# Blocks' first entries read from the input, histogram ahead of the first norm, first chunk's indices loaded by themselves

## The chip, the cores and the metric

One core of a Trainium2 chip runs the whole program. The metric is device time in microseconds. A profiled execution has a time of its own, and all rows shown here come from that one. The engines are TensorE (PE), VectorE (DVE), ScalarE (ACT), GpSimd (POOL) and SyncE (SP). Each has its own instruction stream, and they meet at semaphores. SP, ACT and POOL start DMAs.

## The reference

The input is a table x of 6250 nodes by 256 features and a graph of 206250 edges (src, dst), sorted by dst. One layer is computed:

```python
xn = layernorm(x)
q, k, v = xn @ Wq.T + bq, xn @ Wk.T + bk, xn @ Wv.T + bv      # 8 heads of 32
for every node c: softmax over its edges (r -> c) of q[c] . k[r] / sqrt(32), times v[r], summed
x = x + agg @ Wo.T + bo + linear_attention(xn) @ w_out.T + b_out
x = x + mixture_of_experts(layernorm(x))      # 8 experts, top 1, capacity 977
```

The edge weights are not used.

## The kernel before

Nodes stand in 49 tiles of 128. Edges, padded, stand in 1664 blocks of 128 entries; the 1612 blocks that hold real edges fill dst_d and src_d, copies of the lists in device memory.

**Front.** Each tile of x is normed, transposed, and multiplied by the key, value and query weights. The keys and values go to the table kv_d, one row of 520 numbers per node. Beside that the kernel sorts the nodes by their number of edges, and it does so in steps:

- SP copies dst into dst_d (L273), adds the padding (L276, L277), waits for both (L281) and reads the first entry of every block back into fi_i, 13 columns of 128 (L282). Then come the third group of x rows (L284), weights, and the copy of src.
- DVE norms the first seven tiles (L331), then makes a histogram of the first entries (L342 to L370), with matmuls on PE between. From it L412 gets for every node the block in which its edges begin.
- POOL reads that block for each node: 49 indirect DMAs (L417), which wait for L412 and for dst_d. DVE counts in four portions (L426 to L435) how many entries lie before the node. A portion is taken up when the tile loop has come to the tile in `ROWS_AT`; if its rows have not landed, DVE stands. Then POOL reads the first 64 source indices of each node from src_d, 49 indirect DMAs (L438).
- DVE and PE work out each node's place in the order of degree (L442 to L518). POOL scatters each node's query and indices to that place in qs_d, 49 indirect DMAs (L405), tile c after the query of tile c has been made (L782).

The generator `ranks` holds these steps, and the tile loop (L727) takes two steps of it per tile. After the loop, weights for the second attention are centred (L803).

**Loop.** The sorted tiles are handled in chunks of up to 8 edges per node. A ring of 6 buffers takes the gathered rows. For each chunk POOL issues up to 8 indirect DMAs (L1028) after ACT has copied its indices to ixb (L1091 for the first six, L1164 later) and after PE has freed a buffer (e_fr; L1022). DVE multiplies keys by the query (L1391), sums (L1394), later weighs the values (L1425). PE adds them (L1323) and frees the buffer. ACT does the exponentials (L1175, L1176). In the first stretch of the loop PE and ACT also carry the second attention: PE's first matmul of that part (L1239, keys_values(0, 0)) stands ahead of its first L1323, and it needs xw, a tile of xn_d.

**Between.** When all scatters to qs_d have landed, SP's list is, in this order: the indices of the first 13 tiles (L959), their queries (L960), the 36 other tiles in three DMAs of 1920 KB (L962), 3 numbers of every row for all tiles (L963, 6272 pieces of 12 bytes), and then the first three tiles of xn_d (L969). The last part of the file is the mixture of experts.

Of the kernel before, what the change touches and what calls it, by code (L numbers as in the profile page):

```python
# [16 lines left out]
J = 8  # L17
RING = 6
# [12 lines left out]
QI = 320  # L31
SW = 323
WIDE = 50 * QI + 4 * J * ROW
ROWS_AT = (7, 13, 20, 25)
PUMP = 2
EPS = 1e-5
BIG = 1e30
# [32 lines left out]
def gps_layer_kernel(nc, x, src, dst, wall, ball, wmix, wqm, wout, wo, bo, b_out, gate_w, gate_b, w1, b1, w2, b2, out):  # L70
# [3 lines left out]
    i32 = mybir.dt.int32  # L74
# [5 lines left out]
    V, S, T, G, Y = nc.vector, nc.scalar, nc.tensor, nc.gpsimd, nc.sync  # L80

    ctx = ExitStack()
    with ctx:
        sems = {}

        def sem(name):
            sems[name] = Sem(ctx.enter_context(nc.semaphore(name)))
            return sems[name]
# [12 lines left out]
        def take(n):  # L101
            top[0] += n
            assert top[0] <= 53008 - WIDE, top[0]
            return A[:, top[0] - n:top[0]]

        def r3(ap, b):
            return ap.rearrange("p (a b) -> p a b", b=b)

        def dram(name, shape, dt=f32):
            return nc.dram_tensor(name, shape, dt, kind="Internal").ap()  # L110
# [3 lines left out]
        qs_d = dram("qs_d", [NP, SW])  # L114
        dst_d = dram("dst_d", [NBP, 128], i32)
# [7 lines left out]
        wait = Waits()  # L123
# [7 lines left out]
        def g(ins):  # L131
            return sg.inc(ins)

        def dma(eng, o, i, s, **kw):
            return s.inc(eng.dma_start(o, i, **kw), 16)
# [35 lines left out]
        ixb = [take(J).bitcast(i32) for _ in range(RING)]  # L171
# [13 lines left out]
        def temp(n):  # L185
            pre[0] += n
            assert pre[0] <= 2048
            return R3[:, pre[0] - n:pre[0]]
# [12 lines left out]


        S.preload_act_table_set("natural_log_exp_and_others")
        t_c = g(G.memset(ident, 0.0))
        t_c1 = g(G.memset(tri, 1.0))
        t_c2 = g(G.memset(ones, 1.0))
# [32 lines left out]
        xbuf = [r3(R2[:, o:o + 1792], 256) for o in (12352, 6400, 8192)]  # L239
# [11 lines left out]
        t_x = {0: load_x(0, S)}  # L251
# [8 lines left out]
        t_x[1] = load_x(1, S)  # L260


        s_pad, s_ed, s_fi = sem("s_pad"), sem("s_ed"), sem("s_fi")
        zero = R3[:, 2048:2176]
        blank = R3[:, 3136:3136 + 4 * HR]
        bigi = R3[:, 128:256].bitcast(i32)
# [9 lines left out]
        dma(Y, flat(dst_d)[E:E + 86].rearrange("(a b) -> a b", a=1), bigi[0:1, 0:86], s_ed)  # L276
        t_ed = dma(Y, dst_d[NB:NBP, :], bigi[0:NBP - NB, :], s_ed)  # L277
        assert E + 86 == NB * 128
        firsts = temp(13)
        fi_i = temp(13).bitcast(i32)  # L280
        wait(Y, t_ed)  # L281
        t_fi = dma(Y, fi_i, dst_d.rearrange("(a p) j -> p a j", p=128)[:, :, 0], s_fi, allow_slow_non_contiguous=True)  # L282

        t_x[2] = load_x(2)  # L284
        s_w2 = sem("s_w2")
# [14 lines left out]
        def spread(xt, js):  # L300
            for i in js:
                last = v(V.bn_stats(st[:, 6 * i:6 * i + 6], xt[:, i, :]))
            wait(V, last)
            for i in js:
                v(V.bn_aggr(mv[:, 2 * i:2 * i + 2], st[:, 6 * i:6 * i + 6]))
# [6 lines left out]
        def root(n):  # L312
            wait(S, (sv, sv.n))
            return inverse_root(rs[:, 0:n], r3(mv, 2)[:, 0:n, 1])
# [7 lines left out]
        def norm(xt, n, o=None):  # L322

            spread(xt, range(n))
            wait(V, root(n))
            for i in range(n):
                last = center(xt, i, o)
            return last

        wait(V, t_x[0])  # L330
        t_n = {(0, 6): norm(xbuf[0], 7)}  # L331


        NB13 = 13
        hs = R0[:, 3584:5120]
# [84 lines left out]
        def ranks():  # L420
            for i, (c0, c1) in enumerate(QUARTERS):
                while tile[0] < ROWS_AT[i]:
                    yield
# [251 lines left out]

        wait(V, t_w)
        v(V.tensor_scalar(out=W[:, :, 512:768], in0=W[:, :, 512:768], scalar1=32.0 ** -0.5, scalar2=None, op0=ALU.mult))
        t_bl = v(V.tensor_scalar(out=bal[:, 512:768], in0=bal[:, 512:768], scalar1=32.0 ** -0.5, scalar2=None, op0=ALU.mult))  # L680
# [46 lines left out]
        for t in range(NT + 3):  # L727
            tile[0] = t
            grp, j = divmod(t, 7)
# [39 lines left out]
            if 0 <= t - 2 < NT:  # L769
                u = t - 2  # L770
                b0, b1_ = ps[2 * (u % 2)], ps[2 * (u % 2) + 1]
# [6 lines left out]
            if 0 <= t - 3 < NT:  # L778
                u = t - 3
                b0, b1_ = ps[2 * (u % 2)], ps[2 * (u % 2) + 1]  # L780
# [71 lines left out]
        e_arr = [esem(f"arr{i}") for i in range(RING)]  # L852
# [5 lines left out]
        e_xs, e_ix, e_q = [esem(n) for n in ("xs", "ix", "q")]  # L858
# [1 line left out]
        e_kv, e_ke, e_k1, e_k2, e_k3, e_ks, e_kz, e_dz, e_wm = [esem(n) for n in  # L860
            ("kv", "ke", "k1", "k2", "k3", "ks", "kz", "dz", "wm")]
        e_xw = [esem(f"xw{i}") for i in range(3)]
        s_in = [sem(n) for n in ("s_ids", "s_first", "s_others", "s_sorted3")]
        sortedi = r3(sorted3.bitcast(i32), 3)
        s_ag = sem("s_ag")
        e_so, e_si, e_sa, e_sd, e_se, e_sl, e_sg = [esem(n) for n in ("so", "si", "sa", "sd", "se", "sl", "sg")]
# [82 lines left out]
        def _(e):  # L949
            p, u, bs, last = regs(e, "y_", ["p", "u", "bs", "last"], [0, 0, 0, 0])  # L950
# [5 lines left out]

            e.wait_ge(s_q.h, s_q.n)
            some_rows = lambda a_, b_, c0, c1: qs_d[a_ * 128:b_ * 128, c0:c1].rearrange("(t p) w -> p t w", p=128)
            s_in[0].inc(e.dma_start(qi[:, 0:FIRST, 256:QI], some_rows(0, FIRST, 256, QI)), 16)  # L959
            s_in[1].inc(e.dma_start(qi[:, 0:FIRST, 0:256], some_rows(0, FIRST, 0, 256)), 16)  # L960
            for c0, c1 in ((FIRST, 25), (25, 37), (37, NT)):
                s_in[2].inc(e.dma_start(qi[:, c0:c1, :], some_rows(c0, c1, 0, QI)), 16)  # L962
            s_in[3].inc(e.dma_start(r3(sorted3, 3), some_rows(0, NT, QI, SW), allow_slow_non_contiguous=True), 16)  # L963
# [116 lines left out]
        def _(e):  # L1080
# [4 lines left out]
            e.nop().then_inc(e_bc, 1)  # L1085
            e.nop().then_inc(e_ks, 1)
            e.wait_ge(sv.h, t_rg[0][1])
            e.wait_ge(s_in[0].h, 16)
            for k in range(RING):
                e.reg_load(ix_, nsl[0:1, 52 + k:53 + k])  # L1090
                e.activation(ixb[k], ixf[:, bass.ds(val(e, ix_, NT * QI + 320 - J), J)], ACT.Copy).then_inc(e_ix, 1)  # L1091
            e.wait_ge(sv.h, t_wm[1])
# [775 lines left out]
```

## Time and profile before

| | us |
|---|---|
| median of 3 runs | 2860.02 (2859.44 to 2861.61) |
| the profiled execution | 2859.73 |
| its span, first to last instruction | 2858.5 |
| outside the span | 1.2 |

| stage | from, us | to, us |
|---|---|---|
| front: tiles, histogram, order | 0 | 212.6 |
| from the last scatter to the first gather | 212.6 | 219.8 |
| gathers | 219.8 | 2291 |
| scatters of the attention's output | 2291.6 | 2354.2 |
| mixture of experts | 2354.2 | 2858.5 |

A row of the timeline gives the start, the duration, the engine, the line, what is done to which tensor, and in brackets how long the engine was idle before it and what ended that. The waits view sums such idle times by the line that waited and what it waited for: the total, the number, the longest. A view of one line gives the shortest, median and longest time of its DMAs from issue to landing. The DMA view splits a stretch by queue: q1 is SP's, q10 is ACT's, q0 is POOL's.

### The profile page before, as it was taken

What the parts mean: (1) busy time and instruction counts of PE and PEld (TensorE: products, weight loads), DVE (VectorE), ACT (ScalarE), POOL (GpSimd) and SP (SyncE); (2) the same over time, 40 slices, a digit from 0 to 9 for tenths busy, and PEclk for the clock granted to TensorE, in tenths of its full rate; (3) what the DMA queues carried; (4) which work ended last, traced back from release to release, by engine and by line L of the source; (5) the groups of instructions that cost most, each with busy time, mean ns of one, the idle gap of its engine ahead of it and who ended that gap; (6) DMA issues with size and microseconds to landing.
All of it is one profiled execution on the core that took longest, in us unless ns stands there. A gap on an engine that the chain in (4) does not pass through costs nothing. (4 is left out here: it accounts for less than half of the span.)

```text
span 2858.5 us, 36150 instructions
## 1 busy us (share of the span) xinstructions
PE 2101.6 (74%) x9360; PEld 1688.3 (59%) x9361; DVE 2399.5 (84%) x3265; ACT 1026.7 (36%) x4371; POOL 2104.4 (74%) x2222
## 2 busy tenths in 40 slices
PE   6872777777877777777888766666566537599998
PEld 5752665655666565555666554444444427499997
DVE  6774999988989999999999888899999956366765
ACT  3422666665666666211111110101111105335453
POOL 5776777777777777777777777777777775578785
PEclk9985999999889999889999887878887875699999
DMA  7759777777777777878888877777777749333331
GB/s 248 270 206 294 221 219 217 219 217 218 219 217 219 218 219 216 244 231 258 256 256 256 252 223 212 210 211 211 210 211 211 211 154 293 118 76 89 80 90 15
DMA packets 257843, 586.96 MB, mean 205 GB/s; under 512 B 49474, under 2 KB 135569, under 8 KB 257613
## 3 DMA queue, kind: packets, MB, share of 16 engines
q0 software_dynamic: 150448, 467.11, 58.2%
q1 hardware_dynamic: 98027, 109.52, 11.6%
q10 hardware_dynamic: 9296, 9.44, 1.0%
q8 instruction: 37, 0.61, 0.1%
q14 instruction: 35, 0.29, 0.0%
HBM read 519.06 MB, written 71.84 MB: 207 GB/s over the span
## 5 line engine op out<-in xcount | busy, mean ns | idle before, releaser
L1028 POOL DMA_INDIRECT wide<-kv_d,arena x1099 | 1051.3, 957 | 347.4 <-issue 326.1
L1323 PE MATMUL ps<-wide,arena 128*128 128x264 f32 x2432 | 706.8, 454 | 229.2 <-DVE wide L1425 229.0
L1323 PEld LDWEIGHTS ps<-wide,arena 128*128 128x128 f32 x2432 | 539.4, 227 | 389.5 <-DVE wide L1425 273.7
L1028 POOL DMA_INDIRECT arena<-kv_d,arena x539 | 515.7, 957 | 164.3 <-issue 157.9
L1161 ACT ACTIVATE ps<-wide 128x256 f32 x229 | 88.7, 387 | 1262.0 <-DVE arena L1391 1258.3
L1394 DVE TENSOR_REDUCE arena<-arena 128x64 f32<-128x2048 f32 x229 | 523.9, 2288 | 7.9
L1323 PE MATMUL ps<-arena 128*128 128x264 f32 x1216 | 345.7, 446 | 135.0 <-DVE arena L1425 134.9
L1391 DVE TENSOR_TENSOR arena<-wide,ps 128x2048 f32<-128x2048 f32 x153 | 349.4, 2284 | 88.0 <-DMA wide<-kv_d,arena 87.7
L1323 PEld LDWEIGHTS ps<-arena 128*128 128x128 f32 x1216 | 264.3, 222 | 211.8 <-DVE arena L1425 157.4
L140 PE MATMUL ps<-halves 128*128 128x256 f32 (+2 forms) x2304 | 362.1, 319 | 3.1 <-DVE halves L1686 1.6
L1425 DVE TENSOR_TENSOR wide<-wide,ps 128x2112 f32<-128x2112 f32 x152 | 356.8, 2347 | 0.0
L140 PEld LDWEIGHTS ps<-halves 128*128 128x128 f32 x2304 | 331.7, 192 | 31.0 <-POOL halves L1696 3.4
L1239 PE MATMUL ps<-arena 128*128 128x256 f32 x528 | 136.4, 404 | 98.4 <-DMA arena<-xn_d 52.0
L1391 DVE TENSOR_TENSOR arena<-arena,ps 128x2048 f32<-128x2048 f32 x76 | 173.5, 2284 | 34.3 <-DMA arena<-kv_d,arena 34.1
L1131 ACT ACTIVATE arena<-arena 128x64 f32<-128x64 f32 x784 | 197.8, 334 | 3.2
L1425 DVE TENSOR_TENSOR arena<-arena,ps 128x2112 f32<-128x2112 f32 x76 | 178.4, 2347 | 16.2 <-ACT arena L1176 16.2
L1123 ACT ACTIVATE arena<-arena 128x64 f32<-128x64 f32 x784 | 188.7, 242 | 3.1
L1239 PEld LDWEIGHTS ps<-arena 128*128 128x128 f32 x528 | 99.7, 199 | 117.9 <-DMA arena<-xn_d 53.5
L1792 DVE TENSOR_TENSOR halves<-arena,halves 128x978 fp32r<-128x978 f32 x64 | 97.9, 1539 | 65.8 <-ACT halves L1790 65.8
L1123 ACT ACTIVATION_READ_ACCUMULATOR arena<-arena 128x1 f32 x784 | 146.2, 186 | 0.0
L1831 POOL DMA_INDIRECT out<-arena x48 | 80.1, 1668 | 78.3 <-DVE arena L1828 37.8
L140 PE MATMUL ps<-rear_halves,row_halves 128*128 128x512 f32 (+1 forms) x392 | 113.0, 361 | 14.2 <-DVE wide L785 13.1
(337 smaller groups left out, 3079.2 us busy)
## 6 DMA issues: line engine op xcount, KB each, us to landing
wide<-kv_d,arena POOLq DMA_INDIRECT x1099, 3.8
arena<-in_w SPq DMA_DIRECT2D x16, 1024.0 KB, 5.5
kv_d<-wide SPq DMA_DIRECT2D x49, 260.0 KB
arena<-xn_d SPq DMA_DIRECT2D x82, 128.0 KB, 3.5
arena<-kv_d,arena POOLq DMA_INDIRECT x539
hb_d<-arena SPq DMA_DIRECT2D x16, 516.0 KB, 6.7
xn_d<-arena SPq DMA_DIRECT2D x7, 896.0 KB
base_d<-arena ACTq DMA_DIRECT2D x49, 128.0 KB, 3.4
```

The costliest lines, as they stand in the source:

```text
L140: m = T.matmul(o, l, r, start=(first and i == 0), stop=(last and i == len(pairs) - 1))
L1028: e.indirect_dma_start(out=kvb[k][:, j, :], out_offset=None, in_=kv_d, in_offset=bass.IndirectOffsetOnAxis(ap=ixb[k][:, j:j + 1], axis=0)) ...
L1123: m = e.activation(o[:, 64 * h:64 * h + 64], raw[:, 64 * h:64 * h + 64], ACT.Square, accum_out=ssq[:, h:h + 1])
L1131: m = e.activation(o[:, 64 * h:64 * h + 64], raw[:, 64 * h:64 * h + 64], ACT.Copy, scale=rr_[:, h:h + 1])
L1161: return e.activation(q_ps, qsf[:, bass.ds(val(e, qa, NT * QI), 256)], ACT.Copy)
L1239: m = e.matmul(o, xw_[slot][:, i, :], W0[:, i, c:c + 256], start=(i == 0), stop=(i == 1))
L1323: m = e.matmul(psE[(k + 1) % 3][:, 0:264], ident, kvb[b][:, j, 256:ROW], start=(j == 0), stop=(j == J - 1))
L1391: e.tensor_tensor(prod.rearrange("p (j n) -> p j n", n=256), kvb[k][:, :, 0:256], q_ps.unsqueeze(1).to_broadcast([128, J, 256]), ALU.mult) ...
L1394: e.tensor_reduce(S_ps[:, 0:8 * J], prod.rearrange("p (n d) -> p n d", d=32), AX.X, ALU.add).then_inc(e_red, 1)
L1425: e.tensor_tensor(kvv[b], kvv[b], p3.unsqueeze(3).to_broadcast([128, J, 8, 33]), ALU.mult).then_inc(e_pv, 1)
L1792: t_hs[e * 8 + f] = v(V.tensor_tensor(hl[:, f, 0:CE], hf[f % 2], hh[:, f, 0:CE].bitcast(f32), ALU.subtract))
L1831: t_yq[q] = s_ye[q % 4].inc(G.indirect_dma_start(out=out, out_offset=bass.IndirectOffsetOnAxis(ap=rows_[:, jj % 4, 256:257].bitcast(i32), ...
```

## The change

fi_i is filled from the input dst itself: POOL first sets it to 2^20, SP waits for that, and three DMAs with 1536, 75 and 1 entries are the first on SP's list, ahead of the copy to dst_d. SP no longer waits for dst_d. The norm of the first seven tiles stands behind the histogram on DVE. The portions of `ROWS_AT` are taken up at tiles 5, 10, 16 and 21. In the loop's head SP loads the 8 indices of chunk 0 by themselves straight into ixb[0], and ACT only passes the word on. SP then waits until chunk 0's 8 gathers have landed, before it loads the 36 other tiles.

```diff
-ROWS_AT = (7, 13, 20, 25)
+ROWS_AT = (5, 10, 16, 21)
...
+        firsts = temp(13)
+        fi_i = temp(13).bitcast(i32)
+        s_fi = sem("s_fi")
+        t_fm = g(G.memset(fi_i, 1 << 20))
+        wait(Y, t_fm)
+        first_of = lambda b0, n: dst[b0 * 128:(b0 + n) * 128]
+        dma(Y, fi_i[:, 0:12], first_of(0, 12 * 128).rearrange("(a p j) -> p a j", p=128, j=128)[:, :, 0], s_fi, allow_slow_non_contiguous=True)
+        dma(Y, fi_i[0:75, 12:13], first_of(1536, 75).rearrange("(p j) -> p j", j=128)[:, 0:1], s_fi, allow_slow_non_contiguous=True)
+        t_fi = dma(Y, fi_i[75:76, 12:13], dst[206208:206209].rearrange("(a b) -> a b", a=1), s_fi)
         t_c = g(G.memset(ident, 0.0))
...
-        firsts = temp(13)
-        fi_i = temp(13).bitcast(i32)
-        wait(Y, t_ed)
-        t_fi = dma(Y, fi_i, dst_d.rearrange("(a p) j -> p a j", p=128)[:, :, 0], s_fi, allow_slow_non_contiguous=True)
...
-        wait(V, t_x[0])
-        t_n = {(0, 6): norm(xbuf[0], 7)}
-
...
+        wait(V, t_x[0])
+        t_n = {(0, 6): norm(xbuf[0], 7)}
         wait(V, t_w)
...
             some_rows = lambda a_, b_, c0, c1: qs_d[a_ * 128:b_ * 128, c0:c1].rearrange("(t p) w -> p t w", p=128)
+            s_in[4].inc(e.dma_start(ixb[0], qs_d[0:128, 256:256 + J].bitcast(i32)), 16)
             s_in[0].inc(e.dma_start(qi[:, 0:FIRST, 256:QI], some_rows(0, FIRST, 256, QI)), 16)
             s_in[1].inc(e.dma_start(qi[:, 0:FIRST, 0:256], some_rows(0, FIRST, 0, 256)), 16)
+            e.wait_ge(e_arr[0], 16 * J)
...
+            e.wait_ge(s_in[4].h, 16)
+            e.nop().then_inc(e_ix, 1)
             e.wait_ge(s_in[0].h, 16)
-            for k in range(RING):
+            for k in range(1, RING):
```

## Rows read from the trace of the kernel before

**Rows 1.** Waits of POOL, whole span: line and what it waited for, total, times, longest

```profile
POOL wide L1028 <- issue: 326.1, 1070, 0.3
...
POOL wide L1028 <- PE ps L1323: 11.3, 19, 5.8
```

**Rows 2.** Timeline of POOL at the places where its run of DMAs starts, breaks and ends

```profile
22.23 1.29 POOL L417 DMA_INDIRECT arena<-dst_d,arena  x1 [17.65 <-DVE arena L413]
...
211.60 0.97 POOL L405 DMA_INDIRECT qs_d<-wide,arena  x1 [0.30 <-issue]
219.80 0.99 POOL L1028 DMA_INDIRECT wide<-kv_d,arena  x1 [7.23 <-ACT arena L1091]
...
268.93 0.95 POOL L1028 DMA_INDIRECT wide<-kv_d,arena  x1 [0.30 <-issue]
275.72 0.95 POOL L1028 DMA_INDIRECT wide<-kv_d,arena  x1 [5.84 <-PE ps L1323]
...
2353.19 0.97 POOL L1075 DMA_INDIRECT at_d<-wide,arena  x1 [0.30 <-issue]
```

**Rows 3.** Timeline from 262 us to 277 us, the loop's head: first of PE, then DVE

```profile
266.33 3.78 PE L1239 MATMUL ps<-arena 128*128 128x256 f32 x8 [51.96 <-DMA arena<-xn_d]
...
276.07 2.35 DVE L1425 TENSOR_TENSOR arena<-arena,ps 128x2112 f32<-128x2112 f32 x1 [16.18 <-ACT arena L1176]
```

**Rows 4.** Timeline of the first 23 us: waits and ends of norm and histogram

```profile
6.84 2.39 DVE L302 BATCH_NORM_STATS2 arena<-wide 128x6 f32<-128x256 f32 x7 [0.83 <-DMA wide<-in_x]
...
10.45 3.11 DVE L319 TENSOR_SCALAR wide<-wide,arena 128x256 f32<-128x256 f32 x7 [0.61 <-ACT arena L310]
11.49 0.40 SPq L135 DMA_DIRECT2D arena<-dst_d  x1
...
15.16 0.17 DVE L343 TENSOR_SCALAR arena<-arena 128x13 int32<-128x13 int32 x1 [1.60 <-DMA arena<-dst_d]
...
21.86 0.42 DVE L679 TENSOR_SCALAR wide<-wide 128x512 f32<-128x512 f32 x1
```

**Rows 5.** Timeline around the rows of the first nodes and the last query

```profile
68.77 0.39 DVE L767 TENSOR_TENSOR row_halves<-arena,row_halves 128x256 fp32r<-128x256 f32 x1
...
71.67 0.95 POOL L417 DMA_INDIRECT arena<-dst_d,arena  x1 [0.31 <-issue]
...
201.50 0.38 ACT L782 ACTIVATE wide<-ps 128x256 f32<-128x256 f32 x1 [2.21 <-PE ps L140]
```

**Rows 6.** Timeline from 214 us to 235 us: first loads, first indices, first product

```profile
214.19 0.37 SPq L959 DMA_DIRECT2D wide<-qs_d  x1
...
215.44 18.63 SPq L962 DMA_DIRECT2D wide<-qs_d  x3
218.70 0.21 ACT L1091 ACTIVATE arena<-wide 128x8 int32 x1 [16.81 <-DMA wide<-qs_d]
...
234.69 2.29 DVE L1391 TENSOR_TENSOR arena<-wide,ps 128x2048 f32<-128x2048 f32 x1 [20.09 <-DMA wide<-kv_d,arena]
```

**Rows 7.** Issue to landing: L1028, L417, L962

```profile
DMA to landing us min/median/max: 3.4/3.8/6.6
...
DMA to landing us min/median/max: 2.4/5.0/7.2
...
DMA to landing us min/median/max: 18.7/28.5/35.2
```

**Rows 8.** DMA by queue, 4 us each from 216, 220, 232, 256: packets, MB, share

```profile
q1 hardware_dynamic: 2183, 1.27, 111.6%
...
q1 hardware_dynamic: 1274, 1.42, 108.6%
...
q0 software_dynamic: 255, 0.86, 57.6%
q1 hardware_dynamic: 514, 0.65, 46.7%
...
q1 hardware_dynamic: 3304, 0.06, 48.4%
```

More of the change, by code:

```diff
@@ L260, in gps_layer_kernel @@
         t_x[1] = load_x(1, S)
-        s_pad, s_ed, s_fi = sem("s_pad"), sem("s_ed"), sem("s_fi")
+        s_ed = sem("s_ed")
         zero = R3[:, 2048:2176]
@@ L862, in gps_layer_kernel @@
         e_xw = [esem(f"xw{i}") for i in range(3)]
-        s_in = [sem(n) for n in ("s_ids", "s_first", "s_others", "s_sorted3")]
+        s_in = [sem(n) for n in ("s_ids", "s_first", "s_others", "s_sorted3", "s_ids0")]
         sortedi = r3(sorted3.bitcast(i32), 3)
```

## The prediction

> **What bounds the kernel now.** I first ask which engine never rests, and read the waits of POOL over the whole span. Nearly all its idle time in the gathers is "issue", never longer than 0.3 us at a time; the one long wait for PE is the 5.8 us inside 19 waits of 11.3 us in all [rows 1]. So the gathers are a run of 1638 DMAs, one each 1.26 us, which nothing but a late start or a break can lengthen. The timeline of POOL shows where the run starts and breaks [rows 2]: it starts at 22.23 with the first row gather, goes on without a gap through 3 x 49 DMAs to 211.60 + 0.97, stands 7.23 us, does 40 gathers (five chunks) from 219.80 on, stands 5.84 us before 275.72, and then runs to 2353.19 + 0.97, beyond which the experts follow. There are three idle pieces: 22.2 us, 7.2 us and 5.8 us. The change works on the first two.
>
> The third decides whether that counts. At 268.93 POOL issues the last gather of chunk 4, and the sixth chunk's buffer must be freed by PE. So I go to what PE waits for in the loop's head: its first L1239 starts at 266.33 after 51.96 us of waiting for a tile of xn_d [rows 3]. PE's list has that matmul ahead of the first L1323, so no buffer is freed until it is done. From 266.33 it is 9.39 us to POOL's restart at 275.72, and 9.74 us to DVE's L1425 at 276.07, which had stood 16.18 us behind ACT's L1176, which is behind the same matmul [rows 2, 3]. The tile of xn_d is the last thing on SP's list, behind 5.90 MB of sorted tiles. Everything ahead of 266.33 is thus covered by that load: the time moves by what the landing of that load moves, and by nothing else that happens before.
>
> **The change, part by part.**
>
> *First entries and histogram.* Before, DVE stands 1.60 us for fi_i and begins the histogram at 15.16; POOL starts 7.07 us later, at 22.23 [rows 2, 4]. After, the three small DMAs are SP's first. The trace has none like them; the old read took 15.16 - 11.49 = 3.67 us from issue with 1664 such entries [rows 4], and the x rows, issued at about 0.9, were used from 6.84 with the same neighbours. Issued at 1.3 to 2.5, the third lands between 2.5 + 3.67 = 6.2 and some 8. DVE's constants end at 6.0, so I take 6.5. Then POOL starts at 6.5 + 7.07 = 13.57, 8.66 us earlier. It also needs dst_d, which landed by 11.49 [rows 4]; its copy is now behind three DMAs of about 0.4 us issue each, so 11.5 to 13, hidden by the 13.57. The memset ahead of POOL's constants costs 0.1 to 0.2 us, hidden under the same wait. Behind SP's removed wait stood the third x group, the weights and the copy of src; they go out some 4 us earlier beside x group 1, and none is waited for then. Between gain and loss of 1 us: 0.
>
> *Norm behind the histogram.* The norm takes 10.45 + 3.11 - 6.84 = 6.72 us, of which 0.61 is ACT's root. It now ends at about 13.3 + 6.7 = 20.0, and L679 comes at 20.1 instead of 21.86: the two idle pieces of DVE, 0.83 and 1.60, are gone, less 0.7 [rows 4]. The tiles come 1.8 us earlier, or 0 to 1.8.
>
> *ROWS_AT.* The rows must have landed when the tile loop comes. The tightest is tile 16: before, DVE came there after the L767 at 68.77, now at about 67.4; the 39th row gather went out at 71.67, now at 63.0, and lands 5.0 (median) to 7.2 us later, 68.0 to 70.2 [rows 5, 7]. DVE may stand 0.6 to 3 us. Behind it on DVE are the tiles. The last query was done at 201.9 [rows 5]; with -1.8 and up to +3 it is at 200 to 203, and the last scatter, now due at 211.60 - 8.66 = 202.94, has it, or waits at most 0.4. The later portions are ready long before POOL comes to them. Cost 0.
>
> *Chunk 0's indices.* From L959 to ACT's L1091 it was 4.51 us with 416 KB, and POOL came 1.10 later; 214.19 is 2.59 us after the last scatter's issue [rows 2, 6]. With 4 KB the landing is no longer than that, and no shorter than the 2.4 us of the fastest row gather [rows 7]. I take 3.0, a saving of 1.5 (0 to 2.1), nearer the lower end because the load is tiny. The other five chunks' indices are copied by 211 and wanted at 219. First gather: 202.94 + 2.59 + 3.0 + 1.1 = 209.6 instead of 219.80.
>
> The Trainium skill, "DMA: Bandwidth & Descriptors", section "Anatomy of one DMA", gives a small DMA a fixed time of about 2.0 us. No row here shows so short a landing, 2.4 being the least; by the page the first gather would be 1 us earlier and so would everything behind it.
>
> *The wait for chunk 0.* SP now holds its list until 8 gathers have landed. The eighth goes out 7 x 1.257 + 0.06 = 8.86 us after the first. Before, DVE had it at 234.69, which is 6.0 us after 219.80 + 8.86, beside the tile loads [rows 2, 6]; the median of all gathers is 3.8 [rows 7]. So the wait ends at 209.6 + 8.9 + 3.8 = 222.3, and DVE's first product comes there instead of 234.69 [rows 6]. Behind the wait are queued: the 36 tiles, the 3 numbers per row, and the xn_d tiles that PE waits for. The 36 tiles start at 222.3 instead of 215.44 [rows 6], 6.9 us later. What do they meet? Between 220 and 224 q1 was alone and moved 1.42 MB in 4 us; between 232 and 236, beside the gathers' 0.86 MB, it moved 0.65 MB (the windows of 4 us from 224 to 252 have 0.65 to 0.71) [rows 8]. Before, q1 had 2.69 MB behind it by 224 (1.27 in the window before that, with the engines just as full), out of 7.60 (5.90 and the first tiles' 1.70). The other 4.91 MB take 4.91 / 0.165 = 29.8 us, to 253.8, and 12.5 us later, after the 6272 small pieces, PE has its tile. After, 5.90 MB begin at 222.3 + 1.3 and go the whole way beside the gathers: 5.90 / 0.165 = 35.8 us, to 259.4. With the same 12.5 us PE starts at 271.9. But now the gathers of five chunks end their issue at 209.6 + 50.3 = 259.9 and land by about 263.7, so the small pieces have the engines to themselves for the second half. In 256 to 260 they ran at 3304 in 4 us beside gathers, and used 48.4% of the engines for it [rows 8]; alone they could go up to twice as fast. That gives back 0 to 3.4 us; I take 1.8, the middle. PE starts at 271.9 - 1.8 = 270.1, that is 3.8 us later than 266.33.
>
> **The sum.** In POOL's run: first idle piece -8.66, second -1.5, third +10.2 + 3.8. The first two come to 10.2 us that the third takes back in full, and 3.8 is added: POOL restarts at 279.5. From there on nothing differs. 2859.73 + 3.8 = 2863.5 us; the median before is 0.3 us over the profiled execution, so the same holds to within that.
>
> Bounds: small entries at 6.2 or 8, indices between 0 and 2.1 saved, small pieces between 0 and 3.4 given back. Lower: -0.3 - 0.6 - 1.6 on the 3.8, with the first bytes 1 us earlier, some +0.3. Upper: +1.5 + 1.5 + 1.8, some +8.6.
>
> **The rivals.**
>
> *Slower, the landing of the anchor.* The later chunk 0 lands, the later the whole list starts: here each us that the front fails to gain is lost one for one in the end. If the small entries crawl behind 900 KB of x, as the first x rows did until 6.84, and dst_d with its padding comes at 17 instead of 11.49, POOL starts at 17.3, the wait on SP ends at 226.0, and PE starts at 273.8: +7.5 us, 2867.2. It decides from a POOL start of about 15.5. For it: SP's and ACT's loads share the engines there, and the first x rows needed until 6.84 [rows 4]. Against: the copy of dst moves in a few large pieces and dst_d was complete 10 us after its issue.
>
> *Faster, the gain goes through.* If the tile of xn_d lands before the five chunks are issued, the third piece is gone: -8.66 - 1.5 - 5.5 = -15.7, 2844.1 us. That needs PE's start at 251 or so, the loads alone at 1.42 MB in 4 us. Against it: the gathers take 0.86 MB of each 4 us [rows 8].
>
> *The same to the microsecond.* The small pieces take all 3.4 us back and the indices the full 2.1: PE starts within 1 us of before, 2859 to 2861. Part of a gain then stays with neither.
>
> *The front does not change.* A histogram bound by something else (POOL start at 22) would put the wait's end at 231 and the time at +12; nothing in the rows shows such a thing, and I give it no chance of its own.
>
> **How the numbers follow.** The forecast, a shift between +0.3 and +8.6 with its middle at 3.8, has 0.66; 0.2% is 5.7 us, about what a measurement can tell from no change, and of the 0.66 some 0.16 lie above it. The slower rival has 0.14, 0.11 of it above 5.7. The faster one has 0.10. The one with no shift has 0.10. Together: faster 0.10, same 0.50 + 0.03 + 0.10 = 0.63, slower 0.27. The range is 2857 to 2869, which leaves out the faster rival and the farthest of the slower.
>
> **What would show it.** Of the changed kernel: POOL's first L417 at about 13.6 with no gap up to a last scatter at about 203; the first gather near 209.6; SP's three large loads from 222.3 on and DVE's first product there; then POOL standing not 5.8 but about 19.6 us before the 41st gather; PE's first L1239 near 270; from there all rows of before moved by the same few us up to the end. If POOL's third piece is short, the middle of the argument, that the xn_d tile is queued behind loads that now start later, is wrong.

## The result, and the profile after

The changed kernel takes 2868.68 us (median of 13 runs, 2865.62 to 2873.93), the kernel before, run in turns with it on the same chip, 2861.61 us (13 runs, 2859.44 to 2863.19). The ratio is 1.0026, with a 95% interval of 1.0018 to 1.0035: slower by 7.1 us. The forecast of 2863.5 us was a shift too small to measure, and what came is slower clear of the interval; the time still lies within the range of 2857 to 2869, at its upper end. The medians and intervals in this document leave out the few executions in the chip's slower state, such as the profiled one of norm_xw at 3429.43 us. The profiled execution after took 2865.62 us, 5.9 us over that of before.

POOL's timeline after, at the places that [rows 2] show of before. A row is start, duration, engine, line, operation, and in brackets the idle time before it and what ended it:

```profile
18.53 1.16 POOL L418 DMA_INDIRECT arena<-dst_d,arena  x1 [13.91 <-DVE arena L414]
...
209.58 0.97 POOL L406 DMA_INDIRECT qs_d<-wide,arena  x1 [1.63 <-ACT wide L785]
212.66 0.97 POOL L406 DMA_INDIRECT qs_d<-wide,arena  x1 [2.12 <-DVE wide L788]
218.52 0.99 POOL L1033 DMA_INDIRECT wide<-kv_d,arena  x1 [4.89 <-PEq L814]
...
283.68 0.95 POOL L1033 DMA_INDIRECT wide<-kv_d,arena  x1 [15.11 <-PE ps L1330]
```

POOL starts 3.70 us earlier than before, where 8.66 were forecast. All of that is gone by the last scatter, which now waits for the queries of the tile loop and comes 1.06 us later than before. The first gather is 1.28 us earlier. The break ahead of the sixth chunk has grown from 5.84 to 15.11 us, and POOL restarts 7.96 us later. From there nothing is made up: the last L1080 is at 2360.38 (2353.19 before, +7.19), and the experts' part gives 1.3 us of it back in this execution.

The loop's head after, as in [rows 3]: first PE, then DVE.

```profile
274.73 3.78 PE L1246 MATMUL ps<-arena 128*128 128x256 f32 x8 [51.29 <-DMA arena<-xn_d]
...
284.46 2.35 DVE L1432 TENSOR_TENSOR arena<-arena,ps 128x2112 f32<-128x2112 f32 x1 [25.84 <-ACT arena L1183]
```

PE's first keys_values comes 8.40 us later, and it waits, as before, for a tile of xn_d. SP's list from the last scatter on, as in [rows 6], shows why. SP issues the three large loads only when the eight gathers of chunk 0 have landed:

```profile
215.48 0.33 SPq L962 DMA_DIRECT2D arena<-qs_d  x1
215.85 0.43 SPq L963 DMA_DIRECT2D wide<-qs_d  x1
216.33 0.80 SPq L964 DMA_DIRECT2D wide<-qs_d  x1
231.16 12.53 SPq L967 DMA_DIRECT2D wide<-qs_d  x3
243.74 11.40 SPq L968 DMA_DIRECT2D arena<-qs_d  x1
255.55 16.72 SPq L974 DMA_DIRECT2D arena<-xn_d  x2
```

The bulk starts at 231.16 instead of 215.44 and PE has its tile 43.57 us later. DVE has its first product at the same moment, 231.27, 3.4 us earlier than before; it gains nothing, since it then stands 25.84 us at L1432.

Of the first 25 us, DVE's timeline answers [rows 4]:

```profile
11.47 0.17 DVE L344 TENSOR_SCALAR arena<-arena 128x13 int32<-128x13 int32 x1 [5.41 <-DMA arena<-in_dst]
...
18.16 0.42 DVE L307 BATCH_NORM_STATS2 arena<-wide 128x6 f32<-128x256 f32 x1
...
25.02 0.41 DVE L682 TENSOR_SCALAR wide<-wide 128x512 f32<-128x512 f32 x1
```

The first entries are there at 11.47, not at 6.5. The histogram then takes the forecast 7.06 us to POOL's start. The norm stands behind it, and L682 comes at 25.02 instead of 21.86: 3.16 us later, where 1.8 us earlier was forecast. The last query (L785, before L782) is made at 211.52 instead of 201.50.

### The profile page after: what moved, and what is told of

Same layout as the page of the kernel before. It is cut to its first block and busy times, and to the rows that moved or that the text cites. A ratio compares the mean times of both kernels' runs of the same rounds, so it can differ in the third digit from the quotient of the medians.

```text
span 2864.4 us, 36153 instructions
## 1 busy us (share of the span) xinstructions
PE 2107.3 (74%) x9360; PEld 1692.3 (59%) x9361; DVE 2398.2 (84%) x3265; ACT 1026.1 (36%) x4370; POOL 2101.9 (73%) x2223
## 3 DMA queue, kind: packets, MB, share of 16 engines
q1 hardware_dynamic: 98135, 109.52, 11.5%
## 5 line engine op out<-in xcount | busy, mean ns | idle before, releaser
L1432 DVE TENSOR_TENSOR wide<-wide,ps 128x2112 f32<-128x2112 f32 x152 | 356.7, 2347 | 0.0
L1432 DVE TENSOR_TENSOR arena<-arena,ps 128x2112 f32<-128x2112 f32 x76 | 178.3, 2346 | 25.8 <-ACT arena L1183 25.8
```

What stands on the lines that cost most here:

```text
L1432: e.tensor_tensor(kvv[b], kvv[b], p3.unsqueeze(3).to_broadcast([128, J, 8, 33]), ALU.mult).then_inc(e_pv, 1)
```

## The experiments

All are read against the kernel before, run in turns on the same chip. "Bulk" is the issue of the first of the three large loads, "PE" the first keys_values, "restart" the first gather of the sixth chunk. Times are medians; the other columns are read from one profiled execution each, in us. Of norm_xw only the times are used. The last four ran once each, so their times are single runs beside one of the kernel before.

| kernel | time, its before | ratio, interval | last scatter | first gather | bulk | PE | restart |
|---|---|---|---|---|---|---|---|
| before (profiled) | | | 211.60 | 219.80 | 215.44 | 266.33 | 275.72 |
| changed (profiled) | 2868.68, 2861.61 | 1.0026, 1.0018 to 1.0035 | 212.66 | 218.52 | 231.16 | 274.73 | 283.68 |
| head_only | 2866.88, 2859.95 | 1.0024, 1.0015 to 1.0034 | 212.44 | 217.79 | 230.38 | 274.33 | 282.54 |
| front_only | 2861.71, 2859.95 | 1.0007, 0.9998 to 1.0017 | 212.12 | 220.76 | 216.16 | 268.47 | 276.80 |
| before_wait | 2870.47, 2859.69 | 1.0040, 1.0026 to 1.0053 | 211.58 | 219.90 | 232.54 | 276.25 | 285.81 |
| before_ids | 2863.99, 2859.69 | 1.0015, 1.0006 to 1.0024 | 210.88 | 216.19 | 215.43 | 271.42 | 279.68 |
| after_nowait | 2865.51, 2859.47 | 1.0024, 1.0014 to 1.0033 | 211.28 | 217.42 | 215.76 | 271.42 | 280.62 |
| before_xw | 2854.09, 2859.95 | 0.9981, 0.9972 to 0.9990 | 210.44 | 218.86 | 217.77 | 222.39 | no break |
| after_xw | 2853.70, 2859.95 | 0.9981, 0.9972 to 0.9990 | 214.74 | 220.92 | 235.27 | 233.30 | no break |
| after_hold | 2861.96, 2859.47 | 1.0011, 1.0002 to 1.0020 | 205.75 | 211.59 | 224.30 | 268.76 | 278.05 |
| after_rows | 2863.46, 2859.47 | 1.0015, 1.0006 to 1.0024 | 207.75 | 213.98 | 226.56 | 270.20 | 278.30 |
| norm_xw | 2848.30, 2859.47 | 0.9962, 0.9949 to 0.9976 | | | | | |
| best1 | 2848.78, 2859.69 | 0.9960, 0.9947 to 0.9974 | 207.53 | 213.52 | 215.61 | 224.72 | no break |
| best2 | 2844.11, 2859.69 | 0.9947, 0.9934 to 0.9961 | 201.28 | 206.75 | 209.25 | 219.28 | no break |
| after_r18 | 2866.55, 2857.55 | single run | 213.09 | 218.96 | | | |
| after_r16 | 2863.33, 2857.55 | single run | 207.37 | 212.67 | | | |
| after_r21 | 2864.70, 2860.38 | single run | 209.86 | 215.81 | | | |
| after_r25 | 2866.13, 2860.38 | single run | 210.43 | 216.26 | | | |

One profiled execution has a scatter of its own. In the five kernels with the old front and the old ROWS_AT (before, head_only, before_wait, before_ids, before_xw) POOL starts between 22.23 and 23.90 and the last query is made between 200.76 and 203.59; in the four with the whole changed front (changed, front_only, after_nowait, after_xw) between 18.25 and 18.53, and between 210.14 and 213.60. A difference of 3 us or less in the last query, between two single traces, may be that scatter.

### Which half of the change costs the time

*head_only*: the kernel before with the loop's head of the changed kernel (chunk 0's own indices and SP's wait).

```diff
+            s_in[4].inc(e.dma_start(ixb[0], qs_d[0:128, 256:256 + J].bitcast(i32)), 16)
...
+            e.wait_ge(e_arr[0], 16 * J)
```

> The kernel before with the changed head alone: chunk 0's indices by themselves, and SP's wait for chunk 0's gathers. Theory A (all ahead of PE's first L1239 is covered, and the list behind SP's wait sets PE's start): in the changed kernel PE came 43.6 us after the end of the wait, and the wait ended 12.6 us after the first gather. Here the first gather should be near 217.2, the wait's end near 229.8, PE's L1239 near 273.4 instead of 266.3: the time is 7 us longer than before, nearly the whole loss of the change. Theory B (the loss comes from the slower front, the tiles being 10 us later): no difference from before within 2 us.

*front_only*: the kernel before with the changed front alone (entries from the input, norm behind the histogram, new ROWS_AT).

> The kernel before with the changed front alone (first entries from the input, histogram ahead of the norm, earlier portions), its head as before. Theory A: the last scatter was 1.06 us later in the changed kernel, so SP's list and all behind it start 1 to 1.3 us later and the time is 1 to 1.5 us longer. Theory B: the front carries the loss, 5 us and more longer.

The head alone has the whole loss: +6.9 us, and its PE is at 274.33 against 274.73 in the changed kernel (0.8 of its 8.0 us come from a late last scatter: in that execution POOL, whose part is unchanged, started at 23.90). The front alone is +1.8 us with an interval that takes in no change (1 to 1.5 us were expected): it moves the last scatter by half a microsecond, although POOL starts at 18.36 instead of 22.23.

### The two parts of the head, apart

*before_wait*: the kernel before with SP's wait alone. *before_ids*: with chunk 0's own indices alone.

```diff
+            e.wait_ge(e_arr[0], 16 * J)
             for c0, c1 in ((FIRST, 25), (25, 37), (37, NT)):
```

> The kernel before with SP's wait for the eight gathers of chunk 0 ahead of the 36 tiles, nothing else. My theory: first gather at 219.8 as before, the wait ends 12.7 us later at 232.5, PE's first keys_values comes 43.6 us behind that at 276 instead of 266.33, POOL's break grows to about 15.5 us, time +9.5 us, ratio 1.0033. Rival (a list that starts later meets fewer gathers and catches up most of it): PE before 271, time +0 to +4.

> The kernel before with chunk 0's indices loaded by themselves straight into ixb[0], nothing else. My theory (in the kernel before, the bulk load has the engines to itself until the gathers start, and each us that gathers start earlier costs it about one): first gather near 217.4 instead of 219.80, PE's first keys_values 3 to 5 us later than 266.33, POOL's break ahead of the sixth chunk grows from 5.8 to 11 or more, time +3 to +5 us. Rival (the break only grows by the 2.4 us that the gathers start earlier, the bulk load being limited by its own queue): PE at 266.3, time unchanged.

The wait costs 10.8 us by itself, where 9.5 were expected: it ends at 232.54, and PE comes 43.71 us behind. The other part also came as expected, and the next paragraph explains it: a first gather that comes 3.6 us sooner (0.7 of it from an earlier last scatter) makes the kernel 4.3 us slower. The two do not add up: together, in head_only, they cost 6.9 us. Once the list waits for the gathers, an earlier first gather also starts the list earlier.

*after_nowait*: the changed kernel without SP's wait.

> The changed kernel without SP's wait for chunk 0's gathers; chunk 0's indices still by themselves. Theory A (the wait alone moves the list on which PE waits): the three large loads start right behind the first tiles' queries, near 217 instead of 231.2 (215.4 before), PE's L1246 comes 51 us later, near 268, POOL's gap shrinks from 15 to 8 us, and the time is 1.5 to 2 us over before instead of 7. Rival (what the wait costs, the undisturbed gathers give back): no difference to the changed kernel.

This expectation missed. The time is 6.0 us over before, where 1.5 to 2 were expected, and the interval overlaps that of the changed kernel (+7.1): its rival, no difference, came nearer. So in the changed kernel the wait itself costs little; without it the early gathers cost nearly as much. The bulk load starts at 215.76, where it stood in the kernel before, and yet PE is at 271.42, 5.1 us later than there. The DMA view by queue of the stretch from 220 to 224 us says why, first of this kernel, then of before_ids (packets, MB, share of the 16 DMA engines; q1 is SP's queue, q0 POOL's):

```profile
q1 hardware_dynamic: 902, 0.93, 70.8%
q0 software_dynamic: 152, 0.53, 36.0%
```

```profile
q0 software_dynamic: 229, 0.79, 54.2%
q1 hardware_dynamic: 682, 0.70, 51.9%
```

In the kernel before, q1 was alone in that window and moved 1.42 MB [rows 8]. Here the gathers have begun 2.4 us earlier (3.6 in before_ids), and q1 moves 0.93 and 0.70 MB. In the window before that it moved 1.20 and 1.25 (1.27 before). The shortfall of 0.56 and 0.74 MB, made up beside the gathers at the forecast's 0.165 MB a microsecond, is 3.4 and 4.5 us; PE was 5.1 us later in both. The view of the load's line agrees: its third DMA was issued at 222.5 and landed 35.2 us later, at 257.7, in the kernel before, and at 227.6 + 35.1 = 262.7 here and 227.8 + 35.1 = 262.9 in before_ids, so the whole delay lies in the 36 tiles. Most of the cost is of this kind, and 1.7 and 0.6 us stay unexplained. As long as the anchor is the tile of xn_d behind 5.90 MB, a microsecond by which the gathers begin earlier while the load does not is lost in the load, and somewhat more than it.

### The anchor itself

*before_xw*: the kernel before with the three loads of xn_d issued ahead of the 36 tiles, nothing else. *after_xw*: the same with the changed kernel, ahead of the wait too.

```diff
             for i in range(3):
                 mix_in(i)
+            for c0, c1 in ((FIRST, 25), (25, 37), (37, NT)):
+                s_in[2].inc(e.dma_start(qi[:, c0:c1, :], some_rows(c0, c1, 0, QI)), 16)
```

> The kernel before, with the three loads of xn_d tiles moved ahead of the 36 sorted tiles in SP's list; nothing else. Theory A: PE's first L1239 comes near 226 instead of 266.3, POOL's 5.8 us gap before the sixth chunk is gone, and the time is 5.5 us shorter than before (ratio 0.998). Theory C (the sixth chunk's buffer is held by something else, DVE or the ring itself): the gap stays and the time with it.

> The changed kernel, with the same three loads ahead of SP's wait and of the 36 tiles. Theory A: its 15.1 us gap of POOL before the sixth chunk is gone, 14.8 us less than the changed kernel; against before what is left is the first gather 1.3 us earlier and the 5.5 us gap gone, 6.8 us shorter. Theory B (slower front): it stays above before.

PE's row in before_xw shows the long wait gone:

```profile
222.39 3.78 PE L1239 MATMUL ps<-arena 128*128 128x256 f32 x8 [8.70 <-DMA arena<-xn_d]
```

Its waits view (total, times, longest) shows that no gather waits for PE longer than 0.3 us, where it was 5.8 [rows 1]:

```profile
POOL wide L1028 <- PE ps L1323: 3.7, 12, 0.3
```

That is worth 5.9 us to the kernel before, the 5.84 us of its third idle piece, and some 13 us to the changed one (+7.1 us against its own runs of before, and -6.3 with the loads moved). after_xw came within 0.6 us of its expectation, though in its profiled execution the front was 2 us late. The two settle the middle of the forecast: what PE waits for is not work, but its place in SP's list.

### Why the first entries came at 11.5

*after_hold*: the changed kernel, but ACT's loads (x rows and weights) wait until the first entries have landed.

```diff
+        wait(S, t_fi)
         t_x = {0: load_x(0, S)}
```

> The changed kernel, with ACT's loads of x and the weights issued only after the first entries have landed. Theory D (the 1612 four-byte pieces take turns one for one with ACT's packets of 1 to 3 KB, which is why they came at 11.4 instead of 6.5): alone they land near 5, the histogram begins at 6.1 when DVE's constants are there, POOL's first L418 is near 13.2 instead of 18.5, the tiles come 5 us earlier than in the changed kernel, and so does the end: 2 us over before. Rival E (four-byte reads take 9 us by themselves): DVE's wait for the entries ends at 10 or later and all is 4 us later still, since x now comes behind.

DVE then has the entries at 5.98 without a wait, and POOL starts at 12.98. The time is 4.6 us less than the changed kernel's (+2.5 us over before, not +7.1). POOL's row:

```profile
12.98 1.16 POOL L419 DMA_INDIRECT arena<-dst_d,arena  x1 [8.36 <-DVE arena L415]
```

By themselves the pieces are quick. In after_hold the DMA view by queue from 2 to 4 us has nothing but SP's small packets, and from 4 to 6 us there are none left:

```profile
q1 hardware_dynamic: 1644, 0.01, 45.6%
```

In the changed kernel itself the DMA view by queue from 6 to 8 us, and then from 8 to 10, shows SP's small pieces (q1) beside ACT's loads (q10):

```profile
q10 hardware_dynamic: 251, 0.72, 95.9%
q1 hardware_dynamic: 252, 0.00, 7.1%
...
q10 hardware_dynamic: 428, 0.62, 93.5%
q1 hardware_dynamic: 431, 0.00, 12.2%
```

In these two windows the pieces of 4 bytes go one for one with packets of 1.4 to 2.9 KB. In other windows they did not: from 2 to 4 us it was 105 of q1 beside 425 of q10, from 4 to 6 us 709 beside 541. What after_hold shows is that the company of ACT's loads is what made them late. The Trainium skill, "DMA: Bandwidth & Descriptors", section "Queues, rings and completion order", says that a DMA engine goes round between the queues with work, one packet from each; the counts of these two windows agree with it, those of the others less so, and the forecast should have used it. The old read of as many entries, issued at 11.49 in the kernel before, was held up less: from 12 to 14 us q1 sent 1315 packets there beside 460 of q10, which used 64.4% of the engines, and not the 93 to 98% of the changed kernel from 4 to 10 us.

### What ROWS_AT did

*after_rows*: the changed kernel with the old ROWS_AT.

```diff
-ROWS_AT = (5, 10, 16, 21)
+ROWS_AT = (7, 13, 20, 25)
```

> The changed kernel with the portions taken up at tiles 7, 13, 20 and 25 again. Theory F (the tiles are 10 us later because DVE stands for rows that have not landed, and because the rank steps then meet other loads): last query near 205, last scatter bound by POOL's own run at 18.5 + 189.4 = 208, and the time 4 us less than the changed kernel. Rival G (the norm behind the histogram and DMA traffic make the tiles late): last scatter stays at 212 and the time too.

The last query is made at 202.73 instead of 211.52, no scatter waits for one any more, and the time is about 3 us less. So of the 10.0 us by which the last query moved, 8.8 are ROWS_AT's. The other 1.2 may be the later norm's, but 202.73 lies within the 200.76 to 203.59 of the old front, so that is not shown. How the earlier places do it was open. The first suspect was the stand at tile 16, DVE's row:

```profile
75.41 1.89 DVE L427 TENSOR_TENSOR arena<-arena,ps 128x1664 bf16<-128x1664 int32 x1 [2.94 <-DMA arena<-dst_d,arena]
```

Behind it PE has nothing to do. The windows of 4 us from 72 us on (busy time and number of PE, PE's weight loads, DVE, ACT, POOL, then the granted clock of PE, DMA share and GB/s), first of the changed kernel, then of after_rows:

```profile
72.00:76.00 4.00, 4.00 (x24) 3.19 (x23) 1.06 (x4) 1.99 (x5) 3.09 (x4) 1.00 1.08 391
76.00:80.00 4.00, 0.60 (x3) 0.39 (x4) 2.40 (x4) 1.56 (x4) 3.09 (x4) 0.79 1.04 407
80.00:84.00 4.00, 4.00 (x13) 3.19 (x13) 3.90 (x11) 0.00 (x0) 3.08 (x4) 0.50 1.03 399
```

```profile
76.00:80.00 4.00, 3.19 (x17) 2.67 (x18) 3.81 (x14) 0.28 (x2) 3.08 (x4) 1.00 1.03 401
80.00:84.00 4.00, 4.00 (x23) 3.25 (x22) 2.80 (x12) 2.78 (x9) 3.08 (x4) 1.00 1.04 400
```

PE was busy for 0.60 of 4 us, its clock fell from 2.4 to 1.2 GHz, and in the next 4 us it did 13 matmuls instead of 23. A short idle time does not always bring that: the same view of the kernel before has PE busy for 1.12 of 4 us, and its clock stays where it was.

```profile
72.00:76.00 4.00, 1.12 (x8) 0.65 (x6) 0.93 (x3) 1.56 (x4) 3.09 (x4) 1.00 1.04 412
76.00:80.00 4.00, 4.00 (x21) 3.25 (x22) 3.46 (x15) 0.98 (x3) 3.09 (x4) 1.00 1.04 403
```

Four single runs ask which portion it is: *after_r18* has ROWS_AT (5, 10, 18, 21), *after_r16* (7, 13, 16, 25), *after_r21* (7, 13, 20, 21) and *after_r25* (5, 10, 16, 25).

> The changed kernel with the third portion taken up at tile 18 instead of 16; by then its rows (landed at 75.4 in the changed kernel) are there, so DVE does not stand. Theory S (the stand of 2.94 us at tile 16 costs itself and, because PE is idle for 3.4 of 4 us behind it, some 3 us more at the lower level of PE's clock): no wait of L427 for a DMA, granted clock 1.00 from 72 to 90 us, last query (211.5 in the changed kernel, 202.7 with the old ROWS_AT) at 205 to 207. Theory P (it is the earlier place of the portions that squeezes the tiles): last query at 209 or later.

> The changed kernel with ROWS_AT (7, 13, 16, 25): the old places but for the third portion, which stays at tile 16. Theory S: DVE stands about 3 us for its rows at tile 16, PE's granted clock falls to about 0.5 behind it, and the last query comes at 207 to 209, 5 to 6 us behind the 202.7 of the old places. Theory P: the stand alone adds at most 3 us and the tiles catch up on it: last query by 204.

> The changed kernel with ROWS_AT (7, 13, 20, 21): of the earlier places only the fourth portion's is kept, behind which the steps of the order (counts, ranks) begin. Theory O (the steps of the order, begun four tiles earlier, take PE and DVE from tiles that then wait for one another): last query at 208 or later (202.7 with the old places, 211.5 with the new), mean granted clock from 100 to 140 us at 0.87 to 0.91 as in the changed kernel, not 0.96. Theory Q (the first three portions carry it): last query by 205.

> The changed kernel with ROWS_AT (5, 10, 16, 25): the fourth portion, and with it the order's steps, back at its old place. Theory O: last query at 203 to 206, 2.5 us of them from the stand at tile 16. Theory Q: last query at 209 or later.

| ROWS_AT | last query ends | mean granted clock 60 to 180 us |
|---|---|---|
| (7, 13, 20, 25), after_rows | 203.1 | 0.97 |
| (7, 13, 16, 25), after_r16 | 205.2 | 0.97 |
| (7, 13, 20, 21), after_r21 | 209.1 | 0.92 |
| (5, 10, 16, 25), after_r25 | 209.7 | 0.94 |
| (5, 10, 16, 21), changed | 211.9 | 0.91 |
| (5, 10, 18, 21), after_r18 | 212.3 | 0.91 |

Each clock is the mean of three windows of 40 us; those of after_r18 are:

```profile
60.00:100.00 40.00, 36.72 (x188) 29.20 (x188) 29.26 (x78) 19.09 (x52) 30.25 (x33) 0.96 0.97 341
100.00:140.00 40.00, 34.80 (x275) 29.11 (x274) 28.76 (x134) 14.04 (x37) 30.40 (x32) 0.87 0.60 204
140.00:180.00 40.00, 35.61 (x210) 26.94 (x208) 32.91 (x154) 13.98 (x38) 30.40 (x32) 0.91 0.57 199
```

Theory S, the stand, fell: without it (L427 waits for nothing in after_r18) the last query is no earlier, and with it alone (2.30 us in after_r16) the cost is 2.1 us, within the scatter of single traces, where 5 to 6 were expected. Its forecast of the clock missed twice: in after_r16 the clock stayed at 1.00 from 68 to 92 us, stand and all, and in after_r18 it fell to 0.57 in the window from 80 to 84 us all the same, behind a window in which PE was busy for 2.39 us. Of the two left neither held alone. The fourth portion by itself costs 6.0 us (in after_r21 theory O was right on the queries, but the clock from 100 to 140 us was 0.96 and not the 0.87 to 0.91 it expected), and the other three by themselves cost 6.6 (it was wrong in after_r25, where theory Q was right), with stands of 1.58 and 3.20 us among them; together it is 8.8. What goes with the late queries is the clock. In the kernels with the old ROWS_AT (before, head_only, before_wait, before_ids, after_rows, best2) its mean over these 120 us is 0.96 to 0.97, in those with the new one (changed, front_only, after_nowait, after_xw, after_hold, best1) 0.89 to 0.93. As an estimate, 0.91 against 0.97 takes 0.06 x 120 = 7 us of full speed from PE, near the delay of 8.8; in after_r25 the same sum gives only 0.03 x 120 = 4 us for 6.6. Whether the slow clock delays the queries, or both come of a PE that is short of work, is only argued, and which step in the tile loop leaves PE without work is still open.

### The gain put together

*norm_xw*: the old ROWS_AT and the old place of the norm, first entries from the input, chunk 0's own indices, no wait of SP, and the loads of xn_d first.

> The changed kernel with the norm ahead of the histogram and the portions at 7, 13, 20, 25 as before, without SP's wait, and the three xn_d loads ahead of the 36 tiles: of the change only the entries from the input and chunk 0's own indices are left. POOL's first row gather should come at 13.6 + 7.1 = 20.7 instead of 22.2, the last query where it was (201.5), the first gather at 20.7 + 189.4 + 2.6 + 3.0 = 215.7 instead of 219.8, no gap before the sixth chunk: 4.1 + 5.5 = 9.6 us under before (ratio 0.9966). If front and head do not add once the third gap is gone, it is 5.5 us under, as the reordering alone.

*best1*: the changed kernel with ACT's loads held as in after_hold, the loads of xn_d first, and no wait of SP. *best2*: the same with the old ROWS_AT.

> The changed kernel with three edits: ACT's x loads wait until the first entries are in, the three xn_d loads stand ahead of the 36 sorted tiles, and SP's wait for chunk 0 is gone. ROWS_AT stays (5, 10, 16, 21). My theory (what is won ahead of the loop passes through in full once PE's first keys_values no longer stands behind the bulk load): last scatter at 205.8 as in after_hold, first gather at about 211.4 (before 219.80: -8.4), no break ahead of the sixth chunk (-5.5), no later break: 13.9 us less than before, ratio about 0.995. Rival (gathers that start earlier meet more of the bulk load, and the gather run is stretched or breaks elsewhere in the first six chunks): the gain is under 8 us, and POOL shows new waits for PE between 260 and 330 us.

> The same as best1 with ROWS_AT at its old (7, 13, 20, 25). My theory: the queries are made about 5 to 8 us earlier and no scatter waits for one; POOL starts at 12.98 and needs its unbroken 189.4 us, so the last scatter is at 202.4 and the first gather at about 208: 12 us before the old one, and with the missing break (-5.5) 17 us less than before, about 2842.5, ratio 0.994, 3 us better than best1. Rival (the last queries are still late, bound by the later norm and not by ROWS_AT): last scatter at 205 or later, the same time as best1.

norm_xw came near what was expected: 2848.30 us, 11.2 under its own runs of before. best2 is the fastest: 2844.11 us against 2859.69, ratio 0.9947 (0.9934 to 0.9961), 0.5% under the kernel before. Of the three idle pieces its timeline of POOL has the first at 12.97 instead of 22.2 us, the second at 4.51 instead of 7.2, and no third:

```profile
12.97 1.16 POOL L419 DMA_INDIRECT arena<-dst_d,arena  x1 [8.36 <-DVE arena L415]
...
206.75 0.99 POOL L1033 DMA_INDIRECT wide<-kv_d,arena  x1 [4.51 <-PEq L815]
```

The waits view says the same of the third:

```profile
POOL wide L1033 <- PE ps L1330: 5.5, 18, 0.3
```

From the trace it should win 219.80 - 206.75 + 5.5 = 18.6 us; the medians say 15.6, against 17 expected. Its profiled execution, 2839.6, was the fastest of its five and 4.5 us under their median, so the trace shows it at its best. best1 fell 3 us short of its expectation: its last queries were later than in after_hold (last scatter 207.53, not 205.75), with DVE standing 1.51 and 2.81 us for rows at tiles 10 and 16.

## Why the prediction was wrong

The forecast gave 0.63 to no measurable change and 0.27 to slower. Slower came. Two steps failed: the landing of the first entries, put at 6.5 us, and the new ROWS_AT, put at no cost. A third, the drain, was priced too high and hid half of them.

**What held.** The reading of what bounds the kernel was right: the gathers are one run with three idle pieces, and everything ahead of PE's first keys_values is covered by the list that ends in the tile of xn_d. The change sent what the first two pieces won back into the third, and the runs with the loads of xn_d first show that this list is the reason. The wait's end behind the first gather (12.7 forecast, 231.16 - 218.52 = 12.64 measured), the histogram's 7.07 us (7.06) and the covered DVE product were right too.

**The landing of the first entries: 6.5 forecast, 11.47 measured.** The estimate took the 3.67 us of the old read [rows 4] as the price beside the x rows. But that read had 1315 packets through beside 460 in its 2 us; the new one went through the thick of ACT's loads, 1497 small packets in the 8 us from 2 to 10 beside 1645 of theirs. This alone is 4.96 us on POOL's start. The slower rival named this ("small entries crawl behind 900 KB of x"), and its figures (POOL's start 17.3, the wait's end 226.0, PE at 273.8, 2867.2 us) are near what came (18.53, 231.16, 274.73, 2868.68), though not by the same terms: it had POOL held by dst_d as well, landing at 17, and POOL's row names only the histogram (L414) as what it waited for; the wait's end was later than it said because of the next step, the drain shorter. So the nearness is partly luck. It had 0.14 and should have had more, since a row that speaks for it, the x rows' landing only at 6.84, was there.

**The norm: 1.8 us earlier forecast, 3.16 later measured.** It stands behind the histogram, so it inherited the entries' delay. What that cost the last query is at most the 1.2 us that after_rows keeps, which is within the scatter of single traces.

**ROWS_AT: nothing forecast, 8.8 us on the last query.** The forecast looked for DVE's stand and found it, 0.6 to 3 us (2.94 measured), but took it as the only way in which a place in the tile loop can cost. It let the tiles slip by at most 3 us, to 200 to 203, and they came at 211.9. By that the queries and no longer POOL's own run set the last scatter: 212.66, where POOL's own run, 189.37 us long as before, would have put it at 207.90 (after_rows has 207.75). That is 4.76 us.

**From the last scatter to the first gather.** 5.86 us instead of 6.69: the indices landed in 2.1 us and not in 3.0. The forecast's floor of 2.4, taken from row gathers, did not hold either (1.5 us in before_ids). The two misses and this make 4.96 + 4.76 - 0.83 = 8.89, and the first gather came 218.52 - 209.6 = 8.9 us after its forecast.

**The drain: 47.8 us forecast from the wait's end to PE, 43.57 measured.** after_hold, after_rows, head_only and before_wait have 44.46, 43.64, 43.95 and 43.71, whatever the bulk's start. The tiles took 35.3 us (the third was issued at 232.5 and landed 34.0 later, at 266.5) where the terms gave 37.1; from there it was 8.2 us to PE instead of 10.7. That 10.7 began with a misreading of the kernel before. The forecast's 7.60 MB leave out the 0.43 MB of the first indices on the same queue, and it put the end of the tiles at 253.8; their third DMA landed at 222.5 + 35.2 = 257.7. So PE followed the tiles by 8.6 us there and not by 12.5, and the 1.8 us to be given back by small pieces running alone were 0.4: the gathers were still under way beside them (0.79 MB from 268 to 272 us). This error ran the other way and hid half of the 8.9: 8.9 - 4.2 = 4.7, and PE is at 274.73 instead of 270.1. With the 0.44 us by which the restart follows PE more closely, POOL restarts 4.2 us later than forecast. The time against its own runs of before moved by 7.1 us where 3.8 were forecast, in the profiled execution by 5.9. That it stayed inside the range is owed to this error, and so to luck.

**How much hung on them.** With entries at 6.5 and no late query, the first gather would be at 202.94 + 5.86 = 208.8, the wait's end at 221.4, and with the 43.6 to 44.5 of the drain as measured PE would be at 265.0 to 265.9: 0.4 to 1.3 us early. That is worked out, not run; the nearest runs are after_hold (entries at 5.98, but new ROWS_AT: +2.5 us) and after_rows (+4.0). So the forecast of no measurable change hung on the two upstream terms, and most of what was missed there came out in the time, as the slower rival said: with the entries' delay taken away the time falls by 4.6 us (after_hold), with the old ROWS_AT by 3.1 (after_rows).

## What to carry to other kernels

Before an edit ahead of a long queue is costed, find what stands last in that queue and who waits for it: moving three small loads ahead of 5.9 MB was worth 5.9 us, and as long as they stood behind, a first gather that came earlier without the load doing so was lost and cost more on top. A wait added on a queue delays the whole list behind it; here it cost 10.8 us alone and gave the engine it served a product that had nowhere to go. Thousands of tiny pieces are cheap only when no other queue sends large packets at the same time, so price them by a row read under the same traffic, not by the same size. And do not move side steps of a tile loop to earlier places on the ground that nobody waits for their data: here that made the last tile 8.8 us later, with one stand of 2.94 us.

## What the runs showed that was not expected

- Tiny pieces beside large packets: 252 and 431 packets of 4 bytes went in 2 us each with 251 and 428 of the other queue, while with the engines free 1644 went in 2 us (after_hold).
- A small load of 4 KB by SP, chunk 0's indices, landed in 2.1 us, and in the other kernels that have it between 1.5 (before_ids) and 2.6 us (after_rows). The view of that one line in the changed kernel:

```profile
DMA to landing us min/median/max: 2.1/2.1/2.1
```

The Trainium skill, "DMA: Bandwidth & Descriptors", section "Anatomy of one DMA", gives about 2.0 us as the fixed part (for DMAs that POOL issues). This load, issued by SP, lies near it, but the 1.5 us are less, so here it is no lower bound.

- Gathers that begin earlier, with the bulk load starting where it did, slow that load by more than they gain: 2.4 and 3.6 us sooner, PE 5.1 us later each time.
- An idle TensorE can be charged twice: 0.60 us of work in 4 us, and then the lower level of its clock (0.50) in the next 4, with 13 matmuls done where 23 were done at 1.00 in after_rows. In the kernel before, 1.12 us of work in 4 us was followed by 1.00. From 60 to 180 us the mean clock was 0.89 to 0.93 with the new places of four DVE steps and 0.96 to 0.97 with the old ones.
